# A macaron transformer block on one core: the second FFN of the first 1024 tokens beside the attention of the last 1024

## What is computed

```python
x = x + 0.5 * ffn(layernorm(x), gate_W, up_W, down_W)     # 4-bit weights, 512 -> 4096 -> 512
x = x + attention(layernorm(x), w_qkv, b_qkv, w_out, b_out)
x = x + 0.5 * ffn(layernorm(x), gate_W, up_W, down_W)     # the same weights again

def attention(x, w_qkv, b_qkv, w_out, b_out):
    q, k, v = heads(x @ w_qkv.T + b_qkv)                  # 16 heads of 32
    scores = q @ k.T / sqrt(32) + causal
    return (softmax(scores) @ v) @ w_out.T + b_out

def ffn(x, gate_W, up_W, down_W):
    gate, up = x @ gate_W.T, x @ up_W.T
    return (gelu_tanh(gate) * up) @ down_W.T
```

## Time and profile before

| | |
|---|---|
| median of 3 runs | 3143.39 us (3142.69 to 3145.57) |
| the profiled execution | 3144.05 us |
| its span, first to last instruction | 3142.2 us |
| mean granted TensorE clock | 0.980 of 2.4 GHz |
| matmuls recorded | 13408 |

### The profile page before, as it was taken

The page is one execution under the profiler, slowest core; times in us unless marked ns, Lnnn a source line. Parts: engine busy times, 40 slices in busy tenths (PEclk is TensorE's granted clock), DMA queues, the critical chain, the costliest instruction groups (busy, mean ns, idle before and its releaser), DMA issues. The chain is left out here.

```text
span 3142.2 us, 40306 instructions
## 1 busy us (share of the span) xinstructions
PE 3002.4 (96%) x13408; PEld 2306.5 (73%) x13408; DVE 1947.2 (62%) x2795; ACT 1266.8 (40%) x2213; POOL 1264.4 (40%) x880
## 2 busy tenths in 40 slices
PE   5999999999999979999999998669999999999999
PEld 3788888888888857666666664548888888888887
DVE  7656656656566474677777773576665566655664
ACT  4322222222222232588888887143222222222222
POOL 4322222222222256577777777343222222222221
PEclk8999999999999989999999999889999999999999
DMA  2000000000000038533323231300000000000001
GB/s 94 21 28 27 27 20 20 27 27 27 20 20 20 1 95 224 146 67 67 67 65 66 63 87 39 117 21 28 27 27 20 20 27 27 27 20 20 27 14 54
DMA packets 123898, 144.37 MB, mean 46 GB/s; under 512 B 71904, under 2 KB 72160, under 8 KB 120480
## 3 DMA queue, kind: packets, MB, share of 16 engines
q1 hardware_dynamic: 123256, 142.70, 16.2%
q10 hardware_dynamic: 552, 0.59, 0.1%
HBM read 105.26 MB, written 38.01 MB: 46 GB/s over the span
## 5 line engine op out<-in xcount | busy, mean ns | idle before, releaser
L60 PE MATMUL psum<-ffn_x_high,ffn_w_high 128*128 128x512 f32 x2048 | 803.4, 392 | 18.6 <-DVE ffn_gelu L388 18.6
L525 POOL TENSOR_TENSOR ffn_inner<-ffn_gelu,ffn_inner 128x512 fp32r<-128x512 f32 x256 | 345.9, 1351 | 1156.8 <-ACT ffn_inner L470 1156.8
L61 PE MATMUL psum<-ffn_x_low,ffn_w_high 128*128 128x512 f32 x2048 | 799.2, 390 | 0.0
L62 PE MATMUL psum<-ffn_x_high,ffn_w_low 128*128 128x512 f32 x2048 | 798.9, 390 | 0.0
L1327 POOL TENSOR_TENSOR probs_low<-probs,probs_high 128x512 fp32r<-128x512 f32 x384 | 483.7, 1284 | 172.2 <-ACT probs_high L1288 171.6
L378 DVE SCALAR_TENSOR_TENSOR ffn_gelu<-ffn_gelu,psum 128x512 f32<-128x512 f32 x256 | 175.9, 687 | 599.9 <-ACT ffn_gelu L463 599.8
L724 DVE TENSOR_REDUCE chunk_max<-psum 128x1 f32<-128x512 f32 (+3 forms) x640 | 370.2, 606 | 161.3 <-PE psum L706 81.2
L60 PEld LDWEIGHTS psum<-ffn_x_high,ffn_w_high 128*128 128x128 f32 x2048 | 386.2, 189 | 104.0 <-DVE ffn_gelu L388 21.9
L61 PEld LDWEIGHTS psum<-ffn_x_low,ffn_w_high 128*128 128x128 f32 x2048 | 386.0, 188 | 82.0 <-issue 2.0
L62 PEld LDWEIGHTS psum<-ffn_x_high,ffn_w_low 128*128 128x128 f32 x2048 | 385.9, 188 | 80.6
L60 PE MATMUL psum<-ffn_inner,ffn_w_high 128*128 128x512 f32 x1024 | 398.6, 389 | 0.2
(11 more groups left out here) (124 smaller groups left out, 3978.4 us busy)
## 6 DMA issues: line engine op xcount, KB each, us to landing
ffn_words<-packed SPq DMA_DIRECT2D x96, 256.0 KB
ffn_word_scales<-scales SPq DMA_DIRECT2D x96, 256.0 KB
qk_parts<-parts SPq DMA_DIRECT2D x32, 512.0 KB, 4.4
queries<-qk_parts SPq DMA_DIRECT2D x48, 256.0 KB, 4.6
keys<-qk_parts SPq DMA_DIRECT2D x48, 256.0 KB, 6.7
v_parts<-parts SPq DMA_DIRECT2D x16, 512.0 KB, 6.1
values<-v_parts SPq DMA_DIRECT2D x16, 512.0 KB, 11.0
o_parts<-heads_out SPq DMA_DIRECT2D x64, 128.0 KB
```

The costliest lines, as they stand in the source:

```text
L60: pe.matmul(out, w_high, x_high, start=first, stop=False, skip_group_check=True)
L61: pe.matmul(out, w_high, x_low, start=False, stop=False, skip_group_check=True)
L62: return pe.matmul(out, w_low, x_high, start=False, stop=last, skip_group_check=True)
L525: pool.tensor_tensor(inner[:, tb % 2, m, 1, :], product[m], f32(inner[:, tb % 2, m, 0, :]), ALU.subtract)\
```

## The change

The tokens are worked in two halves after `project_in`.

1. `ffn_first` is the first FFN with one addition: SP stores the high and low parts of every weight piece to DRAM (`w_parts`, 96 pieces of 2 x 512 KB), and ACT waits for that store before it overwrites a buffer. The second FFN loads them in place of unpacking.
2. `attend_first` does the attention of the first two query blocks (12 slots a head), with the same banks as before.
3. `ffn_second(..., 0, ...)` projects the first half's heads out, does its layernorm and its FFN, all in one block with the attention of the last two query blocks (28 slots a head). Head 0 runs beside the layernorm, and then each of 15 iterations runs one head beside one FFN group: 24 units of six matmuls are dealt over the 28 slots. The banks are shared: gate 1, up 1, down 2, scores 2, chunks 1, outputs 1.
4. `ffn_second(..., 1, ...)` does out projection, layernorm and FFN for the second half, alone, with 8 banks.
5. A diagonal tile is now multiplied whole in fp32 only where it is at most 256 columns wide; those of 512 and 384 columns are split as the others are.

```diff
-MAX_BANKS = 3
-WHOLE = [t for t in range(SLOTS) if TILES[t][1] >= 4 * TILES[t][0]]
+        self.whole = [t for t in range(self.slots) if self.width(t) <= TB // 2]
+    def __init__(self, half, per_loop, ahead, ring, score_banks, max_banks, first_chunk_slot, chunk_slots, rows_after):
+        self.chunk_slot = [first_chunk_slot + m * chunk_slots // self.slots for m in range(self.slots)]
+FIRST_PLAN = Plan(0, 3, 4, 6, 3, 3, 0, 7, 4)
+SECOND_PLAN = Plan(1, 2, 3, 4, 2, 1, 5, 20, 3)
...
+    def wait_for_max_bank(self, pe, hv, h, item):
+        p = self.plan
+        before = len(p.items) * h + p.items.index(item) - p.max_banks
...
+        (kind, j), h = p.items[before % len(p.items)], before // len(p.items)
...
+            pe.wait_ge(self.max_taken, self.count(hv, h, p.slots, j + 1))
...
+            def iteration(j, s):
+                for t in range(plan.slots):
+                    chunks = plan.chunks_of_slot(t) if has_next else []
+                    scores_ahead(hv, h, t, has_next)
+                    for m in chunks[:1]:
+                        heads.max_chunk(pe, hv, h + 1, m)
+                    if t in UNIT_AT:
+                        unit(j, s, UNIT_AT[t])
+                    heads.with_values(pe, hv, h, t)
+                    for m in chunks[1:]:
+                        heads.max_chunk(pe, hv, h + 1, m)
+                    if has_next and t in plan.rows_at:
+                        heads.rows(pe, hv, h + 1, plan.rows_at[t])
...
+            if heads is not None:
+                max_items(-1)
+            pe.wait_ge(wo_low_ready, 1)
+            for i in range(len(STEPS)):
+                project(i)
+                if heads is not None:
+                    max_items(i)
```

More of the change, by code:

```diff
@@ L1194, in _, with stores, load @@
-            store(HEADS - 4, 3, [2, 3])
-            for i in range(2):
-                sp.wait_ge(out_stored[i], 32 * (HEADS * NTB // 2 + 1))
+            def stores(hv, h):
+                for b in plan.blocks:
+                    heads.store_block(sp, o_parts, sums, hv, h, b)
+            def load(hv, h):
+                heads.load_qk(sp, hv, h)
+                heads.load_values(sp, hv, h)
+            load(0, 2)
+            with sp.Fori(0, loops - 1) as hv:
+                for h in range(plan.per_loop):
+                    stores(hv, h)
+                    load(hv, h + plan.per_loop)
@@ L1262, in _ @@
+            head(loops, last, False)
         @block.vector
         def _(dve):
[L1264 to L1274 removed]
@@ new lines, in _ @@
+            for first, end in released:
+                sp.sem_clear(range(first, end))
+            sp.dma_start(inverse_all[:], row_sums(sums)).then_inc(sums_loaded, 16)
+            if heads is not None:
+                heads.load_qk(sp, 0, 0)
+            sp.dma_start(wo[:], w_out).then_inc(wo_loaded, 16)
+            for i in range(2):
+                load_step(i)
+            sp.dma_start(out_bias[:], b_out).then_inc(bias_loaded, 16)
+            sp.wait_ge(inverse_ready, 1)
+            sp.dma_start(row_sums(inverses), inverse_all[:]).then_inc(inverse_stored, 16)
@@ new lines, in _ @@
+            update(1)
+            for t in range(plan.slots):
+                norm_at(t)
+                if heads is not None:
+                    for m in plan.chunks_of_slot(t):
+                        max_item(0, 1, m)
+            dve.wait_ge(n.std_ready, HALF_TBS)
+            dve.memset(signal[:], 0.0).then_inc(down_free, ND)
+            for q in (2, 3):
+                cube(0, -1, q)
+                gate(0, -1, q)
+                multiply(0, -1, q)
+            with dve.Fori(0, loops) as j:
+                for s in range(2):
+                    iteration(j, s)
@@ new lines, in _ @@
+            if heads is not None:
+                for t in range(plan.ahead):
+                    heads.exps(act, 0, 0, t)
+            for t in range(plan.slots):
+                if heads is not None and t - 1 == plan.last_of_block[0]:
+                    heads.take_out(act, 0, 0, plan.blocks[0])
+                norm_at(t)
+                if heads is not None:
+                    attention_at(0, 0, t, True)
+            for q in (2, 3):
+                take_square(0, -1, q)
+                take_tanh(0, -1, q)
+                inner_high(0, -1, q)
```

1329 lines of the change are left out of this document (868 added, 461 removed).

## The result

The changed kernel takes 3372.4 us (3371.0 to 3373.9) against 3144.5 for the kernel before beside it: ratio 1.0725, 95% interval 1.071 to 1.074, so 7.3% slower. Forecast were 3355 and 6.7%. The profiled execution spans 3369.1 us.

A forecast was written before the change was run, and what follows sets the result against it. TensorE, busy 96%, was taken as the bound. Savings of 45 + 7 us and some 60 of old idle time stood against 147 in the loop, about 125 new idle and about 60 in second prologues: 3355 us, 6.7% slower, range 3215 to 3440.

The forecast's parts named there:

- 5 iteration: Loop of one head beside one FFN group: TensorE's work 60.1 us plus 10.5 of waits, 70.6 an iteration.
- item 7: Second half alone, from switch through projection, layernorm and FFN to the end: 605 us, to 3355.
- The step that carried the forecast: Loop: with one chunk bank, the second of two successive chunks waits for the reduction, 0.7 us lost each time.
- the 10.5 us of waits an iteration: Loop: waits on top of TensorE's work, for chunk reductions, the rows matmul's bank and copy, and the single gate bank.
- the list of what would show it: Signs: eight to 12 us of chunk waits, iterations 68 to 73, slow projection steps, first-half FFN block 1250 to 1270 us.
- waits for the score banks: Sign against the forecast: waits of L816 for the exponentials at the top of the list.
- Item 3: Switch, 14 early items and first-half projection: eight steps that cannot overlap, slowed by the clock; 117 us, to 1604.
- Item 4: Head 0 beside the layernorm, 28 chunks through one bank: 67 us, then first gate and up matmuls 12, to 1683.
- eight steps at 3.5 (two buffers ...) 28: Second half's projection: two buffers, each 7 us through DMA, DVE, ACT and POOL, giving 28 us.
- The saving of "45 us": Attention: splitting the 512 and 384-column diagonal tiles saves TensorE 0.7 us for each of 64 blocks.
- item 2: First-half heads: 11.7 us a head on TensorE, taken as 12.2 beside POOL's 10.3; 197 us, to 1487.
- The first rival: Interleaving fills the attention, as weight loads leave a quarter of its 657 us free: 3030 us; chance 3%.

The follow-up runs named there:

- e1: Changed kernel with TensorE issuing a slot's second chunk ahead of its values matmuls where six FFN matmuls stand between the chunks: 3326.6 us, 1.0573.
- e3: Changed kernel with two chunk banks from head 1 on and one down bank instead of two in the loop: 3315.8 us, 1.0542.
- e5: Changed kernel with DVE scaling projection step i+1 ahead of step i's reductions, step 0's scaling staying behind the early items: 3336.5 us, 1.0603.
- e6: Changed kernel with four instead of two step buffers in the second half's projection: 3362.9 us, 1.069.
- e4: Changed kernel with all diagonal tiles multiplied whole in fp32 again, in both halves of the attention: 3393.5 us, 1.079.
- e8: Kernel before with only the 512-wide and 384-wide diagonal tiles of each block split: 3294.0 us, 1.0476.
- e2: Changed kernel with DVE scaling step 0 ahead of the 14 early items and step i+1 ahead of step i's reductions: 3346.5 us, 1.064.

## Why the prediction was nearly right

| item | predicted | measured |
|---|---|---|
| 1 attention starts | 1290 | 1294, first exponential |
| 2 first-half heads end | 1487 | 1489, last low part |
| 3 switch, early items, projection | 117 us | 122: first matmul at 1535, 11 late; eight steps 76 against 80 |
| 4 head 0, first gates | 67 + 12 | 79 + 12, to 1702 |
| 5 iteration | 70.6 | 68.6 |
| 6 last FFN matmul of the half | 2750 with stores | 2743 |
| 7 second half | 605 | 626 |

- That the total came within 17 us owes something to luck. At the start of the loop the walk was 19 us short (1702 against 1683), the loop gave 28 back (14 x 2.0), and item 7 was 21 short again.
- The step that carried the forecast, one chunk bank that costs TensorE 0.7 us wherever two chunks follow each other, was right in mechanism and nearly in size. Of the 10.5 us of waits an iteration, 8.7 were waits of chunks for reductions, and the trace has 8.1; the rows' copy and the gate bank have 0.6 and 0.8 against 1.0 and 0.8; e1 and e3 move the first as it says. The other us is in TensorE's own work: 68.6 less these waits leaves 59.1, an estimate, where the sum had 60.1. Of the list of what would show it, the number of waits, the period, the steps at a low clock and the length of the half (1491 to 2743, 1252 us) all came; waits for the score banks did not.
- Item 3 was right for the reason given (e5). Its early part was short: the keys of head 0 landed later than my 9 us, so the first chunk started at 1510.6 instead of 1501, and at a clock of 0.50 the chunks came 1.58 us apart, not 1.28.
- Item 4 was 12 us short. Its terms were all taken at full clock, and the clock was 0.71 in that window; in e5, with 0.80, the same stage took 4 us less. No experiment took the rest apart.
- Item 7's term "eight steps at 3.5 (two buffers ...) 28" was mis-sized: a buffer comes back only after DVE, ACT and POOL (about 3 us), the issue of three DMAs (1.3 and more) and the trip of the inverse (7.4 to 8.4 from its issue to DVE's use), so two steps take 10 to 12 us. The eight measured 42; e6 shows the cause. The gap ahead of it was 25 us, not 17, and the layernorm 31, not 28.
- The saving of "45 us" on diagonal tiles is the term that was wrong in kind. It assumed TensorE as the bound in every block. e4 puts it at 21, all in the loop, where ACT and POOL have time to spare; in the first half it was next to nothing. The total hid this, and that is luck: item 2 had taken 12.2 us a head by a margin for POOL, and 12.24 was measured. Its terms for TensorE were too high besides. With whole tiles they give 13.1 us a head (11.7 + 2 x 0.7), where e4 has 12.44 with TensorE never idle: the 41.3 us a head from which they were taken held waits too. In the kernel before the same edit costs 148 us (e8).
- The first rival fell as argued: the loop's weight loads are 65% of its window (638 of 978), yet its matmuls start 0.23 us apart wherever nothing is waited for, and TensorE was idle for 82 us (8%) only. By the Trainium skill's measure (Perfetto Trace Analysis, Identifying the Most-Contended Engine) a third would be free, an estimate from these loads; the trace does not bear it out.

## What to carry to other kernels

Before interleaving two stages, count PSUM banks as well as engines: with one bank a producer waits for write, reduction and return (1.25 us here) each time, and a bank taken from the other stage moves the wait there. When serial chains share an in-order engine, put the next step's operand ahead of the side work, but never a wait for a load ahead of work that is ready. And lightening the busiest engine by giving work to the next busiest pays only in the stages where that one has slack: read ACT and POOL block by block, not over the attention as a whole.

## What the runs showed of the hardware

- A DVE cast of 128x4 from SBUF to SBUF stood up to 6.26 us beside an unbroken run of POOL subtractions (e8), while the reduction next to it kept 0.16 or 0.17 us; the same cast takes 0.17 us when POOL stands. A subtraction of two 128x4 operands in SBUF takes 1.2 us instead of 0.16 when it begins under one of POOL's.
- A TensorE gap can cost more than its own length: with 4 us gaps between projection steps most of a step's matmuls start 0.43 us apart (the 1.2 GHz level; mean clock 0.67), and a step without that gap took 5.5 us at a mean clock of 0.88 (e2).
